# State-space slots: the output projection moved in front of the inner products, except for a unit's first tile

## The reference, cut to what matters

```python
proj = jnp.einsum('bsd,ed->bse', x, in_proj_w)          # gate, hBC, dt
xc = conv_general_dilated(hBC, conv_w, causal, depthwise, 4 taps) + conv_b
hBC = silu(xc)                                          # -> hs, Bm, Cm
xch = hs * dt
Y_diag = einsum(Cc, Bc, L, xch)                         # inside a chunk, L = exp(segsum(A_dt))
states = einsum(Bc, decay_states, xch)                  # carried from chunk to chunk
Y_off = einsum(Cc, prev, exp(A_cum))                    # from the state before the chunk
y = Y_diag + Y_off + hs * D
g = y * silu(gate)
out = g * rsqrt(mean(g * g over the group) + eps) * norm_w
return einsum('bsi,oi->bso', out, out_proj_w)
```

## Time and profile before

| | |
|---|---|
| median of 3 runs | 2850.82 us (2847.45 to 2856.72) |
| the profiled execution's own time | 2847.88 us |
| its span, first to last instruction | 2846.1 us |
| mean granted clock of the tensor engine | 0.943 |
| PE busy | 2491.1 us (88%) |
| DVE, ACT, POOL busy | 1837.2 (65%), 1478.0 (52%), 1599.9 us (56%) |

### The profile page before, as it was taken

One profiled execution on the slowest core, in us unless ns is written; L12 is line 12 of the kernel. 1 busy time (PEld: TensorE's weight loads), 2 busy tenths in 40 slices (PEclk: granted clock), 3 DMA queues, 4 the chain that ended last, 5 costly groups with the idle time before them and its releaser, 6 DMA issues. The chain is left out here.

```text
span 2846.1 us, 37992 instructions
## 1 busy us (share of the span) xinstructions
PE 2491.1 (88%) x12920; PEld 1885.0 (66%) x12920; DVE 1837.2 (65%) x3158; ACT 1478.0 (52%) x2851; POOL 1599.9 (56%) x1323
## 2 busy tenths in 40 slices
PE   7977884799799837999999999999999999999948
PEld 3465662444377625887887887877877877877734
DVE  2158755465532455777777778678778778778765
ACT  2212221555232117667668667667766766866703
POOL 0057667444200203776776776777776776777651
PEclk9989996799989958999999999999999999999978
DMA  3013210100110015234334333434334333334210
GB/s 142 0 47 100 74 59 8 60 1 1 47 58 23 34 49 178 92 98 149 104 105 126 111 106 122 129 107 120 111 103 126 109 112 113 118 110 126 76 48 30
DMA packets 143230, 244.00 MB, mean 86 GB/s; under 512 B 28224, under 2 KB 48448, under 8 KB 142784
## 3 DMA queue, kind: packets, MB, share of 16 engines
q1 hardware_dynamic: 143040, 241.58, 27.3%
HBM read 234.18 MB, written 7.34 MB: 85 GB/s over the span
## 5 line engine op out<-in xcount | busy, mean ns | idle before, releaser
L1672 ACT ACTIVATE mix<-mix,sc 128x128 f32<-128x128 f32 x1024 | 310.8, 389 | 5.4 <-DMA mix<-row_cum 5.4
L96 PE MATMUL ps<-s_xt_hi,w_in_hi 128*128 128x512 f32 x640 | 266.9, 417 | 50.2 <-ACT sg L1664 33.3
L1771 DVE SCALAR_TENSOR_TENSOR feat<-ps,chan,feat 128x511 f32<-128x511 f32 (+2 forms) x384 | 283.8, 739 | 10.1 <-ACT feat L1654 8.3
L1883 POOL TENSOR_TENSOR w_in_lo<-w_in_raw,w_in_hi 128x512 fp32r<-128x512 f32 x160 | 216.8, 1355 | 114.9 <-ACT w_in_hi L1629 114.9
L1801 DVE TENSOR_TENSOR y_lo<-y,y_hi 128x512 fp32r<-128x512 f32 x128 | 171.1, 1337 | 162.1 <-ACT y_hi L1688 159.9
L1760 DVE TENSOR_TENSOR mix<-mix,cb 128x512 f32<-128x512 f32 x256 | 271.0, 1063 | 0.0
L1867 POOL TENSOR_TENSOR xend<-xdt,sc 128x384 f32<-128x384 f32 x128 | 106.9, 835 | 280.1 <-DVE xdt L1734 278.5
L98 PE MATMUL ps<-s_xt_hi,w_in_lo 128*128 128x512 f32 x640 | 253.2, 396 | 0.0
L97 PE MATMUL ps<-s_xt_lo,w_in_hi 128*128 128x512 f32 x640 | 251.9, 394 | 0.0
L96 PE MATMUL ps<-s_xt_hi,w_g_hi 128*128 128x512 f32 x512 | 212.0, 414 | 21.1 <-DVE feat L1771 21.0
L1544 PE MATMUL ps<-w_o_hi,y_hi 128*128 128x512 f32 x512 | 207.4, 405 | 5.4 <-DVE y_lo L1801 3.4
(11 more groups left out here) (269 smaller groups left out, 6424.4 us busy)
## 6 DMA issues: line engine op xcount, KB each, us to landing
mix<-row_cum SPq DMA_DIRECT2D x128, 512.0 KB, 5.8
w_in_raw<-in_w_conv_in SPq DMA_DIRECT2D x160, 256.0 KB, 3.1
w_g_raw<-in_w_gate_in SPq DMA_DIRECT2D x128, 256.0 KB, 3.5
ecb<-row_ecum SPq DMA_DIRECT2D x256, 96.0 KB, 3.4
w_o_raw<-in_w_out SPq DMA_DIRECT2D x64, 256.0 KB, 3.0
w<-in_w_c2q SPq DMA_DIRECT2D x16, 768.0 KB, 4.3
w<-in_w_c2q SPq DMA_DIRECT2D x16, 512.0 KB, 3.7
wqkv<-in_w_qkv SPq DMA_DIRECT2D x1, 3072.0 KB, 13.8
```

The lines of the kernel that those rows point to most:

```text
L96: pe.matmul(out, a_hi, b_hi, start=(n == 0), stop=False)
L1672: last = act.activation(m, m, ACT.Relu, bias=sc[:, b, CUM, z, 2 * i + e:2 * i + e + 1], scale=-1.0)
L1771: dve.scalar_tensor_tensor(out=to, in0=ps[:, j % 2, 0:S - back], scalar=chan[:, bb % B, j, K1 - 1 - back:K1 - back], in1=to, op0=ALU.mult, ...
L1883: pool.tensor_tensor(w_in_lo[:, n % RING, :, :], w_in_raw[:, n % RING, :, :], w_in_hi[:, n % RING, :, :].bitcast(F32), ALU.subtract).then_ ...
```

## The change

Before, `project` came behind `gate` in every slot. Now it is called directly behind `projection`, in front of `inside`, `states` and `gate`, except for a unit's first tile (i = 0, slot 8), which stays behind `gate`. The matmuls themselves and all waits inside the steps are the same, and no other engine's program is changed.

```diff
                 if main:
                     projection()
+                bb8, i8 = behind(g, b, k, 8)
+                if i8 is not None and i8 >= 1:
+                    project(bb8, i8)
                 bb, i = behind(g, b, k, 5)
                 if i is not None:
                     inside(bb, i)
                     states(bb, i)
                 bb, i = behind(g, b, k, 3)
                 if i is not None:
                     gate(bb, i)
-                bb, i = behind(g, b, k, 8)
-                if i is not None:
-                    project(bb, i)
+                if i8 == 0:
+                    project(bb8, i8)
                 bb, i = behind(g, b, k, 6)
                 if i is not None:
                     before(bb, i)
```

## The result

| | before | after |
|---|---|---|
| median | 2850.47 us (4 runs, 2847.45 to 2856.72) | 2884.21 us (4 runs, 2883.97 to 2885.22) |
| span of the profiled execution | 2846.1 us | 2883.4 us |
| mean granted clock | 0.943 | 0.944 |

The ratio is 1.0116, 95% interval 1.0099 to 1.0134: slower by 1.2%. The prediction said 2885, range 2862 to 2904. The profiled executions took 2847.88 us before and 2885.22 after, 37.3 apart, where the medians are 33.7 apart.

What follows compares the result with a forecast made beforehand. The tensor engine was taken to pace the stage. Losses of 27.9, 9.0 and 1.6 us less gains of 2.6 and 1.5 gave +34.4 on 2847.88, thus 2882.3; with 2.9 for the median, 2885, range 2862 to 2904.

Steps and rivals of the forecast that it cites:

- Slot 1: Slot 1: transposes wait for VectorE to carry the same slot's state; 0.86 us lost, 15 times.
- The sign that was named for it: Slots 1 and 2: transposes wait 0.6 to 1.0 us for VectorE's state, some 30 times, 25 us in all.
- P of slot 4: Slot 4's conv product: late off delays y and ScalarE's chain up to the releasing SiLU; 1.0 us later, 15 times.
- y_lo: VectorE's low part of y: takes 0.69 us instead of 1.53 because GpSimd is idle at its start.
- rival C: Contention with GpSimd stays and y_lo keeps 1.53 us: 12.6 us more, 2897; chance 0.17.
- Slot 5: Slot 5: the gate product ends later, so the next conv product waits for its SiLU; 0.6 us lost, 15 times.
- Slot 4: First batches: filled tap wait, but SiLU holds next conv product, 0.37 us won, 7 times; second batches: 0.20 lost, 8 times.
- Tail: Tail: output projection fills the 2.00 us wait ahead of the inner products; 1.5 us won, between 0 and 2.
- A: Slots 1 and 2: only the state wait costs, ScalarE's chain isn't made later; +19, about 2870; chance 0.19.
- B: Slot 4: the tap wait is filled and nothing replaces it; 21.0 us and 1.5 in the tail off, 2828; chance 0.08.
- D: Whole kernel: new waits fall where the tensor engine waits anyway; gains and losses within 9 us, 2850; chance 0.05.
- E: New waits drop the clock to 1.2 GHz briefly, up to 3 us per block; some +20, 2905; chance 0.04.

Runs made afterwards that it cites:

- slot 1 alone: Kernel before the change, with the output projection moved early in slot 1 only: 2882.15 us, ratio 1.0101.
- the last experiment: Changed order with the output-weight cuts moved to the same places as in the cuts moved the second time: 2849.15 us, ratio 0.9989 to before.
- slot 4 alone: Kernel before the change, with the output projection moved early in slot 4 only: 2845.95 us, ratio 0.9983.
- the one without slots 1 and 2: Changed kernel, but in slots 1 and 2 (tail too) the output projection stays behind the states: 2853.06 us, ratio 1.0002 to before.
- off first: Changed kernel, with VectorE making off in slot 2 ahead of the taps and xdt: 2888.98 us, ratio 1.0131 to before.
- slot 2 alone: Kernel before the change, with the output projection moved early in slot 2 only: 2861.63 us, ratio 1.0035.
- slot 5 alone: Kernel before the change, with the output projection moved early in slot 5 only: 2863.08 us, ratio 1.0046.
- the y chain freed: As slot 1 alone, plus in slot 2 VectorE makes off first and GpSimd adds it ahead of xend: 2871.57 us, ratio 1.0071 to before.
- the first try of the cuts: Order of before; ScalarE's and VectorE's output-weight cuts moved to other slots, VectorE one slot behind ScalarE: 2845.33 us, ratio 0.9980.
- the SiLU early: As slot 4 alone, first batches only, with ScalarE's gate SiLU there ahead of its clipping of mix: 2848.60 us, ratio 0.9994 to before.
- the cuts moved the second time: Order of before; output-weight cuts moved out of first-batch slots 2 to 8, some VectorE low parts ahead of y_lo in slot 3: 2808.19 us, ratio 0.9852.

## Why the prediction was right, point by point

**Slot 1.** 0.86 predicted, 0.87 measured in both batches, at the place and by the wait that were named. The experiment with slot 1 alone has it by itself (0.91). The sign that was named for it, waits of 0.6 to 1.0 us and 25 in all, came only in part: the trace puts down 30 waits of 0.38, 11.4 us. In starts T is held by 0.63 and B by 0.32. The sentence that O comes "2.85 to 7.5 us earlier" misreads starts as shifts: O starts 2.82 after P now, and started 4.65 (slot 1) and 7.49 (slot 5) after it before.

**P of slot 4.** 1.0 predicted; 20.68 against 19.71 and 19.47 against 18.49, so 0.97 and 0.98. Its mechanism was shown twice: slot 1 alone makes it with slot 2 untouched, and it goes when y comes in time. off came 0.96 later where the text had 1.09, and y_hi's wait grew by 0.95.

**y_lo.** 0.69, so rival C is out for the changed kernel: the mean of all y_lo from 1200 to 2600 us fell from 1.348 to 1.065 us. The Trainium skill ("SBUF — State Buffer", "Who interferes with whom") has the rule that a VectorE instruction with two inputs in SBUF and a GpSimd instruction that reads it hold a shared port in turn; the trace agrees, as GpSimd is idle from 1814.7 to 1817.69 and y_lo at 1815.67 takes 0.69; so does the mixing of the last experiment, 1.66 beside GpSimd's squares and 0.68 behind them.

**Slot 5.** 0.6 predicted, 0.60 measured 15 times, but 1.56 more in the four first batches in which the clock fell.

**Slot 4.** First batches 0.29 won where 0.37 were said. In second batches the step "0.20 lost, 8 times" was wrong: 9.28 against 9.27, nothing. The text took the SiLU as released by G, which it is, but G as ended 8.71 after P. Slot 4 of unit 7, the end of G and the SiLU:

```profile
1843.25 0.39 PE L98 MATMUL ps<-s_xt_hi,w_g_lo 128*128 128x512 f32 x1
```

```profile
1843.68 0.60 ACT L1666 ACTIVATE sg<-ps 128x512 f32<-128x512 f32 x1 [0.26 <-PE ps L98]
```

G starts 5.61 after P (5.70 in the text) and ends 2.88 later (3.02 in the text, from a G that came behind the states), so 8.49 after P; SiLU and semaphore then end where the old order ended, at 9.27.

**Tail.** From its first transposes to the squares it took 37.7 us (2738.05 to 2775.72), 40.5 before (2700.56 to 2741.08): 2.8 won, where 1.5 were taken. But in the tail of before the granted clock was low once (2735.9 to 2739.3) and in that of the changed kernel never; without some 1.6 us for it 1.2 are won by the order.

**The sum.** From P of slot 3 of the first unit (1081.59 and 1082.78) to the last P (2689.62 and 2727.07) the changed kernel needs 36.3 us more: 15 x (0.87 + 0.97) = 27.6, 15 x 0.60 = 9.0, less 7 x 0.29 = 2.0, and 1.8 for the clock (4 x 1.56 in slot 5, less 4.4 for the three in slot 4 of before), 36.4 in all. Ahead of it lie 1.2 us more, in the tail 2.8 less, and behind it 2.7 more, in code that no edit touches: the first P of slot 3 lay between 1081.1 and 1085.1 us in the kernels here. Pipeline and tail together need 33.5 us more, and 34.4 were predicted: 1.6 too much in slot 4 of the second batches, against 0.6 too much won in the first. The clock cancels in them: four low stretches in either kernel, once that of the tail is counted. That 2885 lies 0.8 from 2884.2 is in part luck. The text added 2.9 because the profiled execution of before lay that far under its median; that of the changed kernel lay 1.0 above its own, and 3.9 us of what lies between the two profiled executions fall outside the pipeline and its tail.

**The rivals.** A (the state wait alone, +19) fails with the kernel of slot 1 alone, which A would put 13 us above before and which lies 31 above it. B (faster) fails with slot 4 alone: 5 us of 21. The Trainium skill ("Perfetto Trace Analysis", "Optimization Strategy") advises to look for the gaps of the most contended engine and to let what they depend on come sooner. A gap filled with other work gave 5 us. Moving the cuts out of the way of the dependencies gave 43, of which slot 4, where the gap stood, has 7 x 2.36 = 16.5; the rest lies in slots 3, 7 and 8 of the first batches and in the clock. The rule holds in that second reading. D fails by the result. E, the clock, is true in part, but at 1.6 us each and not 3, and as many stretches were there before; the "1.00 throughout" of the text is a mean over 1400 us that hides three of them.

## What to carry to other kernels

Work moved into a gap of the busiest engine is worth the gap only if what comes next on it isn't released by another engine's queue at the same time; read that queue first, with all that stands ahead in it, on the taking engine as well as on the making one. What moves away from between two dependent steps (here states and transposes) was cover, and its price is read from the length of the chain that it covered. Where one kind of unit is longer than another of the same work (105.1 against 99.9 us), what only the longer one does is the first suspect, and here its right place was where its engine waited longest.

## What the runs showed of the hardware

**Half clock behind a long wait, in some units and not in others.** Before, three of the seven waits of 2.66 us in slot 4 go with a low granted clock, which begins between 0.6 us before the end of the wait and 1.4 us behind it; the windows are the wait, G and what follows, in unit 10 of before:

```profile
2124.00:2127.00 3.00, 0.42 (x2) 0.00 (x0) 3.00 (x6) 0.81 (x2) 0.64 (x1) 1.00 0.83 250
2127.00:2131.40 4.40, 4.32 (x13) 3.45 (x14) 4.25 (x4) 2.92 (x9) 4.32 (x4) 0.65 0.06 22
2131.40:2136.00 4.60, 4.60 (x23) 3.76 (x22) 4.60 (x5) 4.58 (x14) 4.29 (x4) 0.97 0.08 16
```

0.65 is a mixture of the two levels, 2.4 and 1.2 GHz. The matmuls of the stretch lie 0.43 us apart instead of 0.23, and the slot takes 13.20 instead of 11.64, 1.56 us more. In the changed kernel, and in the one without slots 1 and 2, it happens in four of seven conv products of slot 5, behind waits of 2.2 us. With off first it is six of seven there. In slot 4, behind waits of 2.6 to 2.8 us, it is two of seven with slot 1 alone, four with slot 2 alone, five with slot 5 alone and seven with the y chain freed; with the first try of the cuts, four of fifteen in slot 3, behind waits of 1.9 to 2.6 us. There is none with slot 4 alone, although the waits of 2.20 us in front of slot 5 are there as well, none with the SiLU early (waits of 1.9), and none in the pipeline with the cuts moved the second time, in either order, where no such wait is left. So such a wait is there each time, but is not enough, and what else decides stays open. Runs of one kernel differ by up to 14 us (2846.0 to 2860.3 for before beside the first four), which a few such stretches more or less could explain in part; that was not tested.
